# Where the ring loads of two of four stages are issued, and where VectorE's splits stand in the last stage, in a fused cross-attention and feed-forward kernel

## The reference

```python
q = _layer_norm(query, ln1_g, ln1_b)
qh = (q @ wq + bq).reshape(Bq, Sq, H, hd)
kh = (context @ wk + bk).reshape(Bq, Sc, H, hd)
vh = (context @ wv + bv).reshape(Bq, Sc, H, hd)
scores = jnp.einsum('bqhd,bkhd->bhqk', qh, kh) * scale      # masked: context row <= token
probs = jax.nn.softmax(scores, axis=-1)
o = jnp.einsum('bhqk,bkhd->bqhd', probs, vh).reshape(Bq, Sq, Dm)
x = query + (o @ wo + bo)
h = _layer_norm(x, ln2_g, ln2_b)
return x + jax.nn.gelu(h @ w1 + b1, approximate=False) @ w2 + b2
```

## Time and profile before

| | |
|---|---|
| median of 3 runs | 2058.93 us (2058.73 to 2066.78) |
| the profiled execution's own time | 2065.01 us |
| its span | 2063.1 us |
| TensorE busy | 1789.3 us (87%) |
| VectorE busy | 1282.2 us (62%) |
| ScalarE busy | 952.3 us (46%) |
| GpSimd busy | 688.6 us (33%) |
| DMA, mean | 125 GB/s |

### The profile page before, as it was taken

How to read it: one execution, slowest core, us unless ns; L and a number is a source line. 1 busy time by engine, 2 the same in 40 slices (tenths; PEclk the granted TensorE clock), 3 DMA queues, 4 the chain that set the end, 5 groups by cost and what they waited for, 6 DMA issues and landing times.

```text
span 2063.1 us, 33019 instructions
## 1 busy us (share of the span) xinstructions
PE 1789.3 (87%) x12501; PEld 1059.9 (51%) x12501; DVE 1282.2 (62%) x1838; ACT 952.3 (46%) x1341; POOL 688.6 (33%) x592
## 2 busy tenths in 40 slices
PE   6535589898999989798998999899897988989899
PEld 3222346455555645455564555556554655646465
DVE  6756676555676656566676556666675656766632
ACT  5724645435354534445453444545443453535443
POOL 2656334231433324133342324233341314333200
PEclk9767899999999999999999999999998999999999
DMA  7454454555655355556635545564536556453441
GB/s 260 105 143 140 128 145 111 120 115 128 133 139 123 95 130 129 101 128 143 129 92 134 122 118 118 133 138 120 125 104 119 118 127 133 116 128 105 107 138 62
DMA packets 407954, 258.21 MB, mean 125 GB/s; under 512 B 323417, under 2 KB 324993, under 8 KB 407297
## 3 DMA queue, kind: packets, MB, share of 16 engines
q1 hardware_dynamic: 344304, 140.57, 31.8%
q10 hardware_dynamic: 63504, 115.63, 19.2%
HBM read 151.80 MB, written 24.12 MB: 85 GB/s over the span
## 4 chain that ended last, share of the span: by engine, by line
PE 59%; DVE 12%; SPq 9%; DMA 8%; issue 4%; POOL 3%; ACT 3%; DVEq 1%; ACTq 0%; POOLq 0%
PE ff_ps L1689 21%; PE ff_ps L1667 17%; PE at_ps L1436 16%; SPq L512 8%; DMA arena<-norm_hl 5%; PE at_ps L1591 2%; DMA act_T<-norm_hl 2%; PE at_ps L1611 2%; DVE arena L1072 2%; DVE qT L1072 1%; DMA w_sums<-arena 1%; DVEq L1043 1%; DVE stats L1042 1%; POOL rstd L623 1%; DVE arena L1336 1%
## 5 line engine op out<-in xcount | busy, mean ns | idle before, releaser
L1689 PE MATMUL ff_ps<-w_all,arena 128*128 128x512 f16 x3072 | 753.0, 392 | 44.3 <-DVE arena L1072 44.3
L1667 PE MATMUL ff_ps<-arena,w_ring 128*128 128x256 f16 x5376 | 645.1, 277 | 50.4 <-ACT arena L967 22.5
L1667 PEld LDWEIGHTS ff_ps<-arena,w_ring 128*128 128x128 f16 x5376 | 534.0, 99 | 177.2 <-issue 42.4
L1689 PEld LDWEIGHTS ff_ps<-w_all,arena 128*128 128x128 f16 x3072 | 298.7, 100 | 389.0 <-issue 54.0
L967 ACT ACTIVATE arena<-ff_ps 128x512 f32<-128x512 f32 x256 | 151.4, 591 | 493.3 <-PE ff_ps L1667 466.6
L623 POOL TENSOR_TENSOR rstd<-ve,minus_half 128x1 f32<-128x1 f32 x128 | 89.4, 699 | 742.3 <-DVE ve L1047 742.3
L1072 DVE SCALAR_TENSOR_TENSOR arena<-arena,scales 128x512 f16<-128x512 f32 x260 | 227.7, 886 | 35.7 <-ACT arena L973 17.4
L970 ACT ACTIVATE arena<-arena,b1p,scales 128x512 f32<-128x512 f32 x256 | 205.6, 803 | 1.8
L973 ACT ACTIVATE arena<-arena,scales 128x512 f16<-128x512 f32 x256 | 184.8, 722 | 8.4
L702 POOL TENSOR_TENSOR arena<-arena,rsum 128x1024 f32<-128x1024 f32 x64 | 122.2, 1930 | 164.2 <-DVE rsum L1347 164.2
L1436 PE MATMUL at_ps<-act_T,wq_hi 128*128 128x512 f16 x496 | 154.6, 395 | 25.7 <-DMA act_T<-norm_hl 25.7
(11 more groups left out here) (180 smaller groups left out, 2033.8 us busy)
## 6 DMA issues: line engine op xcount, KB each, us to landing
w_ring<-w_sums ACTq DMA_DIRECT2D x441, 256.0 KB, 3.2
x_sb<-in_x SPq DMA_DIRECT2D x64, 256.0 KB, 2.7
out_x<-arena SPq DMA_DIRECT2D x64, 256.0 KB, 3.6
w_sums<-arena SPq DMA_DIRECT2D x4, 1792.0 KB, 7.4
w_all<-in_L_xattn_w SPq DMA_DIRECT2D x4, 1024.0 KB, 13.6
arena<-in_L_xattn_w SPq DMA_DIRECT2D x3, 1024.0 KB, 6.8
arena<-in_L_xattn_w SPq DMA_DIRECT2D x12, 256.0 KB, 5.5
w_ring<-w_sums SPq DMA_DIRECT2D x7, 256.0 KB, 4.3
```

Of the source, the lines that this page charges most:

```text
L1667: last = nc.tensor.matmul(out_ap, w1_ring[:, i, k, s, cols_of], left(1 - par, i, m, k), start=(n == 0 and q == 0 and i in (0, 1, 3)), stop ...
L1689: last = nc.tensor.matmul(ff2_ps[:, t, :], g_pair[j][:, s, at:at + P], m[:, row], start=(begin and i == 0), stop=(end and i == 2))
```

## The change

Two parts. The tables move steps: R for the second pair of tiles and A by one position on ScalarE; on VectorE the fourth normalisation G and R for the first pair of tiles go from stage 2 into position 24, that is behind splits 0 and 2 and the first quarter's sum (L1400) of stage 3, R for the second pair behind split 1, and A for tiles 0 and 1 ahead of N for tiles 2 and 3. And in stages 0 and 2 ScalarE issues ring loads 0, 1 and 2 together with 3 and 4, behind partial sum 2. Stages 1 and 3 keep their places for the loads.

```diff
@@ ACT_PLAN
-    23: [("R", 0)], 24: [("R", 1)], 26: [("M", 0), ("M", 1)],
-    29: [("A", 0), ("A", 1)], 31: [("A", 2), ("A", 3)],
+    23: [("R", 0)], 25: [("R", 1)], 26: [("M", 0), ("M", 1)],
+    28: [("A", 0), ("A", 1)], 30: [("A", 2), ("A", 3)],
@@ DVE_PLAN
-    22: [("O", 0), ("O", 1), ("G", 0), ("O", 2), ("G", 1), ("O", 3), ("G", 2), ("G", 3)],
-    23: [("R", 0)], 24: [("R", 1)],
-    25: [("N", 0), ("N", 1)], 27: [("M", 0), ("M", 1)], 28: [("N", 2), ("N", 3)],
-    29: [("A", 0), ("A", 1)], 30: [("A", 2), ("A", 3)],
+    22: [("O", 0), ("O", 1), ("G", 0), ("O", 2), ("G", 1), ("O", 3), ("G", 2)],
+    24: [("G", 3), ("R", 0)], 25: [("R", 1), ("N", 0), ("N", 1)], 27: [("M", 0), ("M", 1)],
+    28: [("A", 0), ("A", 1), ("N", 2), ("N", 3)], 30: [("A", 2), ("A", 3)],
@@ ScalarE's slot
                         part(0, parts[0])
-                        reload(0)
+                        if d % 2:
+                            reload(0)
...
                         part(1, parts[1])
-                        reload(1, 2)
+                        if d % 2:
+                            reload(1, 2)
...
                         part(2, parts[0])
+                        if d % 2 == 0:
+                            reload(0, 1, 2)
                         reload(3, 4)
```

## The result

| | before | with the change |
|---|---|---|
| median of the runs | 2058.93 us | 1954.5 us (1952.2 to 1967.93) |
| ratio to before | 1 | 0.950 (95% interval 0.945 to 0.956) |
| the profiled execution's own time | 2065.01 us | 1967.93 us |
| its span | 2063.1 us | 1966.0 us |
| TensorE busy | 1789.3 us | 1764.5 us |

A forecast was written before the change was run, and what follows sets the result against it. It took the stretch of probability transposes ahead of V to be bound by DMA. Terms 74 + 22 - 4 + 10 + 13 + 4 = 119 us off 2065.0 gave 1946, less 6.1 for the median: 1940 us, range 1902 to 2034.

The forecast's parts named there:

- The DMA-bound stretch: Stage 2, probability transposes T0 to T3 ahead of V: DMA bounds it, ring loads being a third of it.
- The V term: TensorE's wait for transposed probabilities ahead of the value products: 5.3 of 6.6 us goes in 14 slots, 74 us.
- sharing: Rival: the five held loads take from T3 what the three took; V term nothing, 2032 us; chance 0.19.
- The clock: Nine down matmuls behind each V wait: the slow stretch at lower clock goes, 1.6 us in 14 slots, 22 us.
- ScalarE's block: Five load issues on ScalarE ahead of V's evictions hold them: 0.3 us a slot charged, -4 us.
- Stage 3: Splits moved ahead of the fourth normalisation shorten TensorE's 2.34 us wait: 13 us in the loop's body, 4 over its end.
- nothing moves: Rival: transposes keep their pace, TensorE waits at Q for what stage 3 gains; 2059 us, within 10; chance 0.09.
- Q: Waits for transposed LayerNorm rows ahead of the query products: without stage 0's loads there, 10 of 13.3 us go.

The follow-up runs named there:

- loads_only: The kernel before with only the change's edits to the ring loads, the tables left as they were: 1977.18 us, ratio 0.961.
- hold_stage2: The changed kernel with ring loads 0, 1, 2 held in stage 2 alone, in stage 0 issued at the slot's start: 1984.34 us, ratio 0.964.
- combined: Changed kernel, stage 2's load block behind V's evictions, splits 0 and 2 ahead of the loop's branch, loads 5 and 6 of stage 1 held: 1895.44 us, ratio 0.918.

## Why the prediction was right

*The DMA-bound stretch* was the right reading: the loads alone give 81 of the 102 us, and taking loads out of the stretch shortened V's waits in each of `loads_only`, `hold_stage2`, the change and `combined`.

*The V term (74 us) was mis-sized*: V waits fell by 52.3 us, to 40.6 and not under 25, and 2.9 us a slot remained, not 1.3; in three slots it was over 4 us, the sign that I had set for sharing. Two numbers of the working failed. T1 was taken at 1.86 us of issue, but it took 3.13, and 4.3 to 5.1 in the slots of the odd chunks: loads 5 and 6, issued beside T0, are still being served under T1. In `combined`, without them, T1 took 1.82 us in the same slot and 2.4 to 3.7 in those of the odd chunks. And 4.4 us to landing was taken from a slot without loads; in the changed kernel T3 landed after 5.62, with the block of five issued 2.3 us behind it. The experiments put 12.9 of the remaining 40.6 us on the block and about 18.6 on loads 5 and 6 (28.1 to 9.5). I had let the block start after T3's issue and counted that as clear; clear is only after T3's landing.

*The clock (22 us)* came out at 24.8, but that agreement is luck. Summed over the 14 slots, TensorE's busy time at the lower level fell from 65.6 to 36.0 us in the 22 us from the start of V, and half of that difference is what V's stretch gave, 15 us, not 22: the first half of V still ran at the lower level in six slots. Another 12 us came from stage 3 (23.9 to 0.0 us at the lower level), where the working counted no clock, since the slot it read has nine matmuls in 2.12 us behind the 2.34 us wait; some 3 us were lost behind the longer waits at the branch.

*ScalarE's block (-4 us)*: nothing was held, 0.

*Stage 3 (17 us)*: 14.3. The 2.34 us waits went in all 14 slots, 0.86 us of new wait stands in the body (0.5 taken), and about 4 us after the branch (3 by the working). The branch with its wait comes five times, not seven, and there nothing was gained: 4.1 us on average, against 2.34 and 1.6, together 3.9, before. And the term was booked as if it stood on its own, while alone the tables are worth nothing, as the rival *nothing moves* said: the Q waits and the wait behind the branch grow. With the held loads they are worth something; that Q is the reason is argued, not shown.

*Q (10 us)*: 5.6 in waits. That undersells the loads of stage 0: putting them back costs 28 us, of which the profiled executions show 17.4 in Q waits. The working also misread its row for Q: the 5.57 us of the earlier trace rows run from the start of the last transpose's issue, not from its end, so they compare directly with the median of 4.7.

*Sharing* was no rival but half of a mechanism. It says that a transfer in the stretch costs T3 its service; the runs say that, plus a step when T3 meets the block. The Trainium skill's rule of interleaving (DMA: Bandwidth & Descriptors, section Issuing engines are not separate DMA queues) is borne out by the 12.9 us that a block issued after T3 still took from it. Its other rule, to issue early and wait late (same page, section Rules for kernel authors), did not hold for this kernel: in stage 2 load 0 goes out 9.0 us later than before and loads 1 and 2 4.4 us later, and that made it faster, since they have slack and the transposes beside them have none.

The sum was 119 us against 97: V's waits 21.7 us worse than forecast, Q 4.4 and stage 3 2.7 worse, the clock 2.8 and ScalarE 4 better. That the clock's term looks right hides a part that the working had not got, the clock of stage 3.

## What to carry to other kernels

When a critical transfer runs in a stretch where the DMA engines are full, look at which other transfers in it have slack, and issue them after the critical one has landed, not after it has been issued. A gain found at one wait is only booked once the next wait down the same engine is known to be free; here the same edit of the order was worth 0, 21 or 42 us, depending on where the ring loads and the splits stood. And look at what a loop's branch costs each engine, which differs: here it was over 3 us on VectorE and 0.3 us on ScalarE. Put work of the engine that loses most, where another engine waits for it, ahead of the branch.

## What the runs showed of the hardware

The cost of ring loads beside the transposes, in time, was 49 us for load 0, 58 us for loads 1 and 2 and 71 us for all three, 36 us less than the sum, where the intervals leave some 19 us either way. In V waits the parts nearly add up (42.1 and 33.5, together 69.8 us), so how much of the 36 us is real stays open. Taken in V waits without a collision, a load cost 0.7 us (loads 5 and 6, 18.6 us for two in 14 slots) to 1.5 us (load 0), around the 0.9 us of service of the earlier trace rows.

In the changed kernel VectorE takes its next instruction 3.6 to 4.3 us after the end of the loop's branch (five times), ScalarE, GpSimd and SyncE theirs after 0.20 to 0.27 us. Why VectorE is the exception no run shows.

The granted clock does not follow the length of a wait alone. Two rows of TensorE's timeline of the changed kernel, the first half of V in the slots of chunks 10 and 15:

```profile
1277.39 0.84 PE L1614 MATMUL at_ps<-arena 64*32 64x512 f16 x24 [3.47 <-DMA arena<-norm_hl]
```

```profile
1832.14 1.48 PE L1614 MATMUL at_ps<-arena 64*32 64x512 f16 x24 [2.23 <-DMA arena<-norm_hl]
```

After 3.47 us without work V runs at full rate (0.84 us), after 2.23 us it takes 1.48. What decides it these rows don't show.
